# Moving three batches' attention epilogue and router into the second attention's loop, with a fixed memory region per expert

## The reference

```python
x = x + _L0_xattn_ref(_layernorm(x), ctx, mask)
x = x + _L0_ffn_ref(_layernorm(x), ...)      # 16 experts, top 6
x = x + _L1_xattn_ref(_layernorm(x), ctx, mask, Wq, ..., residual_scale)
x = x + _L1_ffn_ref(_layernorm(x), ...)      # 16 experts, top 2
```

```python
probs = softmax(clip(q @ k.T / 4))           # 16 heads of 16
ctx = (probs @ v).reshape(B, S, H)
delta = rs * (ctx @ Wo.T + bo)
delta = (delta - mean) / sqrt(var + 1e-5) * ln_gamma + ln_beta
...
logits = flat @ router_w.T
scores = softmax(logits)
_, topk_idx = top_k(logits + router_bias, 2)
# topk_scores normalised to sum 1; for every expert e:
#   out += combine[:, e] * ((silu(flat @ Wu[e]) * (flat @ Wg[e])) @ Wd[e])
# and the shared expert: silu(flat @ Su) * (flat @ Sg) @ Sd
```

## Times and profile before

| | us |
|---|---|
| median of 3 runs | 824.03 |
| lowest, highest | 823.6, 827.82 |
| profiled execution | 823.29 |
| its span in the trace | 821.4 |
| PE / DVE / ACT / POOL busy | 704.0 / 537.9 / 396.3 / 127.8 |

### The profile page before, as it was taken

One profiled execution on the slowest core, in us unless ns is written; L12 is line 12 of the kernel. 1 busy time (PEld: TensorE's weight loads), 2 busy tenths in 40 slices (PEclk: granted clock), 3 DMA queues, 4 the chain that ended last, 5 costly groups with the idle time before them and its releaser, 6 DMA issues.

```text
span 821.4 us, 14394 instructions
## 1 busy us (share of the span) xinstructions
PE 704.0 (86%) x5463; PEld 533.1 (65%) x5463; DVE 537.9 (65%) x1080; ACT 396.3 (48%) x555; POOL 127.8 (16%) x109
## 2 busy tenths in 40 slices
PE   5799999896869999999994699999999984675990
PEld 4689888796658888888884344444444444564880
DVE  6765665666676666666676377777777768563553
ACT  2624233333322223333222599999999981223540
POOL 6452625030000000000000000000000002062651
PEclk9999999998989999999998699999999997896995
DMA  7465554635305334343368289999997209023545
GB/s 228 131 220 196 165 217 150 243 113 192 68 22 135 116 91 131 90 120 103 109 131 189 46 171 140 143 145 200 166 220 143 37 2 345 0 75 104 163 138 179
DMA packets 66456, 114.59 MB, mean 139 GB/s; under 512 B 15984, under 2 KB 44272, under 8 KB 65376
## 3 DMA queue, kind: packets, MB, share of 16 engines
q1 hardware_dynamic: 63136, 106.40, 52.1%
q0 software_dynamic: 2256, 6.18, 2.2%
q10 hardware_dynamic: 1008, 1.25, 0.5%
HBM read 78.93 MB, written 31.75 MB: 135 GB/s over the span
## 4 chain that ended last, share of the span: by engine, by line
PE 51%; ACT 17%; DVE 12%; issue 10%; DMA 5%; POOL 2%; SPq 2%; another core or an unknown queue 1%; POOLq 0%; ACTq 0%; DVEq 0%
ACT p L1155 13%; PE ps L602 12%; PE ps L603 12%; PE ps L604 12%; PE ps L976 3%; PE ps L856 2%; PE ps L838 2%; DMA raw<-in_ctxN 2%; PE ps L990 2%; DMA raw<-in_ctxT 2%; PE ps L614 1%; ACT cNh L1054 1%; POOL cTl L574 1%; DVE st L1204 1%; DMA k_lo<-kl 1%
## 5 line engine op out<-in xcount | busy, mean ns | idle before, releaser
L1155 ACT ACTIVATE p<-ps,kbias 128x1024 f32<-128x1024 f32 (+1 forms) x208 | 208.7, 1426 | 1.1 <-PE ps L838 1.1
L1535 DVE TENSOR_SCALAR p<-p 128x1024 f32<-128x1024 f32 (+1 forms) x208 | 144.2, 693 | 57.9 <-ACT p L1155 56.4
L856 PE MATMUL ps<-p,vsl 128*17 128x256 f32 (+1 forms) x1664 | 113.6, 387 | 0.7 <-DVE p L1535 0.7
L838 PE MATMUL ps<-qst,kst 48*128 48x256 f32 (+1 forms) x832 | 99.7, 328 | 14.4 <-DMA qst<-ql 5.9
L838 PEld LDWEIGHTS ps<-qst,kst 48*128 48x128 f32 (+1 forms) x832 | 60.9, 186 | 75.7 <-ACT p L1155 46.3
L1117 ACT ACTIVATE hh<-h 128x512 fp32r<-128x512 f32 x50 | 31.6, 632 | 138.5 <-DVE h L1467 114.7
L602 PE MATMUL ps<-xTh,w_hi 128*128 128x512 f32 x200 | 79.9, 400 | 5.2 <-DVE h L1463 4.4
L604 PE MATMUL ps<-xTh,w_lo 128*128 128x512 f32 x200 | 79.4, 397 | 0.0
L603 PE MATMUL ps<-xTl,w_hi 128*128 128x512 f32 x200 | 79.3, 396 | 0.0
L583 POOL CAST sh_hi<-e_w 128x768 fp32r<-128x768 f32 x2 | 1.7, 828 | 469.0 <-DMA e_w<-in_w 469.0
L856 PEld LDWEIGHTS ps<-p,vsl 128*17 128x17 f32 (+1 forms) x1664 | 37.7, 97 | 37.8 <-issue 4.3
(11 more groups left out here) (277 smaller groups left out, 1464.9 us busy)
## 6 DMA issues: line engine op xcount, KB each, us to landing
kst<-k_hi SPq DMA_DIRECT2D x64, 200.2 KB, 9.0
w_raw<-in_w SPq DMA_DIRECT2D x25, 384.0 KB, 3.1
v_one<-vst SPq DMA_DIRECT2D x4, 1768.0 KB, 9.2
vsl<-v_one SPq DMA_DIRECT2D x4, 1768.0 KB, 16.2
kst<-k_lo SPq DMA_DIRECT2D x32, 200.2 KB, 8.7
raw<-in_ctxN SPq DMA_DIRECT2D x12, 512.0 KB, 5.8
k_hi<-kh SPq DMA_DIRECT2D x24, 256.0 KB, 2.6
k_lo<-kl SPq DMA_DIRECT2D x24, 256.0 KB, 2.9
```

Source lines behind the costliest of these rows:

```text
L838: mm = pe.matmul(ps[0:rows, 2 * (x % RING) + t, c * SEQ:(c + 1) * SEQ], kst[r, job % KSL, c, m * P:m * P + rows], qst[r, b, 2 * g + c, :], ...
L856: mm = pe.matmul(ps[32 * j:32 * j + VW, 6 + job % 2, 0:SEQ], vsl[0:rows, b % 2, at_:at_ + VW], p32[0:rows, x % PBUF, (2 * t + c) * SEQ:(2 ...
L1155: act.activation(p32[0:rows, x % PBUF, :], psf[0:rows, bank * 512:bank * 512 + 1024], ACT.Exp, scale=0.25, bias=kbias[0:rows, col:col + 1] ...
L1535: dve.tensor_scalar(t, t, CLO, CHI, ALU.max, ALU.min).then_inc(p_clip, 1)
```

## The change

For batches 0 to 2 the work between `cx` and the router moves into the loop of the following batch. Functions `between` on TensorE, ScalarE and VectorE put a piece of it at fixed steps `o` of the 52 steps of a batch (`UB`), in the free half of a PSUM bank; `free_again` keeps the attention's products from overwriting it. The router of batch `b` follows one batch later. In the loop GpSimd computes 1/sqrt(var + eps) by three Newton steps from an integer guess (`inverse_root`), so that ScalarE keeps its table. After the loop stand batch 3 (tiles 6 and 7), the logits of batch 2, and the router of tiles 4 to 7.

Rows go to a region of 1024 rows per expert (`CAP`, `first_row`), so that a position doesn't need the other experts' counts: the scatters of batches 0 and 1 (8 of 16) are in the loop. `x_slots` grows from 3968 to 20480 rows; all of it is filled with empty rows beforehand, by 20 DMAs in the first FFN instead of 12 in the loop. Each block's row in memory (`rb_i`) is worked out by five more linked instructions and read into a register by SyncE. The output projection takes fp32 operands as they are, in one matmul where it was three of fp32r. `norm` comes two steps earlier.

```diff
-NORM_AT = 7
+NORM_AT = 5
...
+CAP = NB * SEQ
+NFILL = E + -(-NBLK * P // CAP)
+UB = NG * MT
...
+        def inverse_root(e, b, n):
+            s = slice(2 * b, 2 * b + 2)
...
+            y, yi = rguess[:, s], rguess[:, s].bitcast(I32)
+            link(e.tensor_scalar(nv[:], mv[:, s, 1], EPS, None, ALU.add))
+            link(e.tensor_scalar(yi, nv[:].bitcast(I32), -0.5, 1597463007.0, ALU.mult, ALU.add))
+            for k in range(3):
+                link(e.tensor_tensor(na[:], nv[:], y, ALU.mult))
+                link(e.tensor_tensor(na[:], na[:], y, ALU.mult))
+                link(e.tensor_scalar(na[:], na[:], -0.5, 1.5, ALU.mult, ALU.add))
+                if k < 2:
+                    link(e.tensor_tensor(y, na[:], y, ALU.mult))
+            e.tensor_tensor(rstd[:, s], na[:], y, ALU.mult).then_inc(rs_rdy, 1)
...
@@ SyncE, first FFN
+                    if 1 <= r <= NFILL:
+                        sp.dma_start(xs_d[(r - 1) * CAP:r * CAP, :].rearrange("(p k) d -> p k d", p=P), blank[:]).then_inc(x_zero, 16)
...
@@ SyncE, attention loop
-                if KSL + NG < job <= KSL + NG + 4:
-                    empty_slots(job - KSL - NG - 1)
...
@@ SyncE, slots_in
-                sp.dma_start(xb[:, j % XR, :], xs_d[j * P:(j + 1) * P, :]).then_inc(xb_in[j % XR], 16)
+                row = sp.value_load(rb_i[0:1, j:j + 1], min_val=0, max_val=NFILL * CAP - P)
+                sp.dma_start(xb[:, j % XR, :], xs_d[bass.ds(row, P), :]).then_inc(xb_in[j % XR], 16)
...
@@ GpSimd, beside the attention loop
+            for b in range(NB - 1):
+                pool.wait_ge(dl_mv, 2 * b + 2)
+                inverse_root(pool, b, 0)
+                pool.wait_ge(ln_mv, 3 * NT + 2 * b + 2)
+                inverse_root(pool, b, 1)
+                if b:
+                    rows_out(b, 2 * b - 2, 2 * b)
...
@@ TensorE, loop
+            def between(y):
+                b, o = y // UB - 1, y % UB
...
+                if 0 < b < NB - 1 and o == 36:
+                    ranks(b, t - 2, t, spare)
+                if 0 < b < NB - 1 and o == 10:
+                    logits(b - 1, spare)
+                if 0 <= b < NB - 1:
+                    if o == 13 - 1:
+                        ctx_T(t, 2, spare)
+                    elif o == 23:
+                        ctx_out(t, 0, 2, spare[:, 0:D])
+                    elif o == 24:
+                        ctx_out(t + 1, 1, 2, spare[:, D:2 * D])
+                    elif o == 49:
+                        rows_T(t, 2, spare)
...
@@ ScalarE, loop
+                    if o == 12:
+                        ctx_ev(t, 2, spare)
+                    elif o == 49:
+                        rows_hi(t, 2, spare)
...
@@ ScalarE, after the loop
+            act.activation(std[:, 0:1], eps[:], ACT.Sqrt)
...
+            act.activation(std[:, 0:1], eps[:], ACT.Silu)
+            for j in range(2):
+                rows_hi(t + j, 1, ps[:, 4 + j, :])
...
@@ VectorE, loop: at o = 25 delta, 27 and 28 its statistics, 30 and 32 gamma
+                    elif o == 34:
+                        delta_add(t)
+                    elif o == 35:
+                        delta_add(t + 1)
+                    elif o == 36:
+                        rows_stat(t)
+                    elif o == 37:
+                        rows_stat(t + 1)
+                    elif o == 39:
+                        rows_mean(b)
+                    elif o == 43:
+                        rows(t)
+                    elif o == 45:
+                        rows(t + 1)
+                    elif o == 50:
+                        rows_lo(t, 2, spare)
...
@@ VectorE, after the first shared chunk
+            link(dve.tensor_tensor(big_d[:], big_d[:], nblk_[:].unsqueeze(1).broadcast_to([P, NBLK, E]), ALU.mult))
+            link(dve.tensor_reduce(ob[:], big_d[:], AX.X, ALU.add))
+            link(dve.tensor_tensor(ob[:], blk[:], ob[:], ALU.subtract))
+            link(dve.scalar_tensor_tensor(out=rb_f[:], in0=eb_f[:], scalar=float(CAP // P), in1=ob[:], op0=ALU.mult, op1=ALU.add))
+            dve.tensor_scalar(rb_i[:], rb_f[:], float(P), None, ALU.mult).then_inc(eb_rdy, 1)
```

More of the change, by code:

```diff
@@ L510, in _ @@
             sp.wait_ge(slots_out, 16 * 2 * NT)
+            sp.wait_ge(eb_rdy, 2)
             def slots_in(j):
@@ new lines, in ranks @@
+            def ranks(n, t0, t1, o):
+                pe.wait_ge(sel_rdy, n)
+                pe.wait_ge(tri_rdy, 2)
+                pe.matmul(o[:, 0:(t1 - t0) * E], upper[:], sel[:, t0:t1, :].rearrange("p t e -> p (t e)"), start=True, stop=False, skip_group_check=True)
+                for t in range(t1 - 1):
+                    u = max(t + 1, t0)
+                    mm = pe.matmul(o[:, (u - t0) * E:(t1 - t0) * E].rearrange("p (t e) -> p t e", e=E), ones[:], sel[:, t:t + 1, :].broadcast_to([P, t1 - u, E]),
+                                   start=False, stop=t == t1 - 2, skip_group_check=True)
+                mm.then_inc(pre_rdy, 1)
@@ new lines, in delta_mean, with delta_gamma, delta_add @@
+            def delta_mean(b):
+                dve.wait_ge(dl_st, 2 * b + 2)
+                for t in (2 * b, 2 * b + 1):
+                    dve.bn_aggr(mv[:, t, :], st6[:, t, :]).then_inc(dl_mv, 1)
+            def delta_gamma(t):
+                dve.wait_ge(dl_mv, t + 1)
+                dve.scalar_tensor_tensor(out=dlt[:, t, :], in0=dlt[:, t, :], scalar=mv[:, t, 0:1], in1=gam[:], op0=ALU.subtract, op1=ALU.mult).then_inc(dl_g, 1)
+            def delta_add(t):
+                dve.wait_ge(rs_rdy, t // 2 * 2 + 1)
+                dve.wait_ge(dl_g, t + 1)
+                dve.wait_ge(beta_rdy, t + 1)
+                dve.scalar_tensor_tensor(out=resid[:, t, :], in0=dlt[:, t, :], scalar=rstd[:, t:t + 1], in1=resid[:, t, :], op0=ALU.mult, op1=ALU.add).then_inc(dl_r, 1)
@@ new lines, in rows_stat, with rows_mean, rows @@
+            def rows_stat(t):
+                dve.wait_ge(dl_r, t + 1)
+                dve.bn_stats(st6[:, t, :], resid[:, t, :]).then_inc(ln_stat, 1)
+            def rows_mean(b):
+                dve.wait_ge(ln_stat, 3 * NT + 2 * b + 2)
+                for t in (2 * b, 2 * b + 1):
+                    dve.bn_aggr(mv[:, t, :], st6[:, t, :]).then_inc(ln_mv, 1)
+            def rows(t):
+                dve.wait_ge(rs_rdy, t // 2 * 2 + 2)
+                if t == 0:
+                    dve.wait_ge(q_in[NG], 16 * 3 * HG * NG)
+                    dve.wait_ge(d_cst, 16 * 10)
+                    dve.tensor_copy(xe[:, :, D + 1], tok[:]).then_inc(xe_rdy, 1)
+                dve.tensor_scalar(xe[:, t, 0:D], resid[:, t, :], mv[:, t, 0:1], rstd[:, t:t + 1], ALU.subtract, ALU.mult).then_inc(ln_xn, 1)
@@ L1631, in _ @@
-            dve.tensor_tensor(sel[:], one1[:], one2[:], ALU.add).then_inc(sel_rdy, 1)
-            dve.wait_ge(pre_rdy, 1)
-            cnt = ps[:, 6, NT * E:NT * E + E]
+            b, t = NB - 1, NT - 2
+            for j in range(2):
+                delta(t + j, 1, ps[:, 2 + j, :])
+                delta_stat(t + j)
+            delta_mean(b)
+            delta_gamma(t)
+            delta_gamma(t + 1)
+            dve.wait_ge(rg_rdy, 1)
+            dve.reciprocal(rstd[:, t:NT], std[:, t:NT]).then_inc(rs_rdy, 1)
@@ new lines, in _ @@
+            delta_add(t)
+            delta_add(t + 1)
+            rows_stat(t)
+            rows_stat(t + 1)
+            rows_mean(b)
+            dve.wait_ge(rg_rdy, 2)
+            dve.reciprocal(rstd[:, t:NT], std[:, t:NT]).then_inc(rs_rdy, 1)
+            rows(t)
+            rows(t + 1)
+            for j in range(2):
+                rows_lo(t + j, 1, ps[:, 4 + j, :])
+            logits_ev(t - 2, NT, ps[:, 7, :])
+            biased(t - 2, NT)
+            max_equal(t - 2, NT)
+            max_first(t - 2, NT, one1)
@@ L1759 @@
         "tok": np.arange(NB * SEQ, dtype=np.float32).reshape(NT, P).T,
-        "empty": np.stack([np.full((P, NBLK), 100.0, np.float32), (NB * SEQ + np.arange(NBLK * P, dtype=np.float32)).reshape(NBLK, P).T], axis=2),
+        "first_row": np.tile(np.arange(E, dtype=np.float32) * CAP, (P, 1)),
+        "aside": (NROW + np.arange(NBLK * P, dtype=np.float32)).reshape(NBLK, P).T,
         "upper": np.triu(np.ones((P, P), np.float32), 1),
```

402 lines of the change are left out of this document (247 added, 155 removed).

## The result

The changed kernel takes 816.9 us (median of 4 runs, 815.9 to 818.8) against 825.9 of the kernel before in the same rounds: a ratio of 0.9887, 95% interval 0.9862 to 0.9912. So it is faster by about 1%, 7 to 9 us, where 19 were forecast. The profiled execution took 816.0 with a span of 814.2.

What follows compares the result with a forecast made beforehand. Bounds: ScalarE's exponentials in the second attention's loop, then a 71.4 us serial chain to the experts. Profiled 823.3 - 27.4 (tail) + 8.5 (loop) = 804.4, predicted as 805 us; range 796 to 818.

Steps and rivals of the forecast that it cites:

- rival 1: Loop: VectorE's clips starve GpSimd's inverse root, costing 6 to 12 us in three batches; 812 us; 0.30 together with rival 2.
- I add 1.5: Loop: VectorE's two waits per batch for GpSimd's inverse root, taken as 3.9 us long, cost 1.5 us in all.
- rival 2: Tail: the 6.73 us wait of unknown releaser before the residual add stays; 812 us; 0.30 together with rival 1.
- the cast slowed from 0.67 to 1.07: Kernel's first microseconds: GpSimd cast took 1.07 us beside VectorE, 0.67 without; cited as evidence for rival 1.
- ScalarE's 3.6: Loop: six copies of 128x512 at 0.60 us each, unhidden because ScalarE is the bound, add 3.6 us.
- TensorE's 3.4: Loop: lumps of projections, logits and context transposes overrun the ring of three score buffers, adding 3.4 us.
- gamma 6.2 and add 7.3: Tail: last batch's gamma ends 6.2 us after the loop's end, reciprocal and add 7.3, at 0.34 to 0.41 per VectorE instruction.
- The 16 zero matmuls and the chunk ahead of the ranks, 1.9 + 2.8: Tail: TensorE's zero matmuls take 1.9 us and 12 shared-chunk matmuls 0.23 each, so it reaches the ranks at 18.0.
- up to 3 us for the clock: Tail: up to 3 us may be lost if TensorE is at 1.2 GHz while the shared chunk runs.
- From the positions on: Tail: positions at 20.8 us, then scatters beside shared expert, softmax weights and residual adds; experts start at 44.0.
- Rival 3: First FFN: empty-row fills exceed the 5.0 us free per tile period, costing 26 us; 831 us; chance 0.07.
- Rival 4: More gain: loop costs only ScalarE's 3.6 us and the tail ends 3 us sooner; 797 us; chance 0.08.

Runs made afterwards that it cites:

- e1: Changed kernel with GpSimd's inverse root of the first three batches replaced by a plain multiply: 812.0 us, 0.981 of before; loop 219.8 us.
- e9: Changed kernel with VectorE's statistics, means, adds and rows moved by one or two steps, whole root kept: 811.7 us, 0.983 of before; loop 220.3 us.
- e6: Changed kernel with the inverse root replaced by a multiply and ScalarE's six loop copies cut to 2 or 4 columns: 809.6 us, 0.978; loop 217.6 us.
- e2: Changed kernel with GpSimd's split of the shared weights held until the last normalized rows are written: 814.1 us, 0.986 of before; tail 47.0 us.
- e3: Changed kernel with the 16 zero matmuls issued earlier, where TensorE idles ahead of the last row transposes: 815.5 us, 0.987 of before; tail 46.5 us.

## Why the prediction was wrong

The direction and the range hold (816.9 in 796 to 818), the gain does not: 9 us instead of 19. That the range holds is in part luck: it let the loop run to 22 over before and took the tail as worked out, and the tail was 6.3 us longer. The prediction's own signs said so too: from the first exponential to the end of the last one 222.8 us (205 to 220 foreseen), a tail of 50.3 (42 to 47), and 3.1 us a batch of VectorE idle for rstd, where over 2 was to mean rival 1. By its own steps:

*The loop's "I add 1.5" for the two waits for GpSimd.* This step failed. They cost 7.1 (e1) or 6.7 (e9), 5.7 by the means of six loops each. I priced the root at 3.9 us from uncontended links; it took 5.2 to 6.5 beside the clips, while the rows were asked for after 4. That is rival 1 in kind, and in size (6 to 12 us in three batches), though not in its arithmetic: it had one link per clip and 5.0 us of waits a batch, and the trace has about two links per clip and 3.1 us. I gave it and rival 2 together 0.30. The row that spoke for it, the cast slowed from 0.67 to 1.07, was less to the point than I wrote: the slow one stood beside a VectorE instruction with two SBUF inputs (L1325), not beside a clip, and VectorE worked beside the fast one too (L1312, L1317, L1319). I let VectorE's own waiting outweigh it. That waiting did free GpSimd (the second roots took 5.2 to 5.5 us, the first 6.3 to 6.5), but not enough.

*ScalarE's 3.6 and TensorE's 3.4* were right: 3.8 of copies in the trace, and 3.1 (e6). With the 7.1 they make 14.1 of loop, where it grew by 14.0.

*The tail's gamma 6.2 and add 7.3.* This step failed too: the pairs took 5.2 us together instead of 1.8. I had weighed GpSimd against VectorE for the loop and not for the tail, where GpSimd splits the shared weights at the same moment. In the kernel before, the split was over at 687.0 and gamma began at 690.7. Price 3.4 (e2).

*The 16 zero matmuls and the chunk ahead of the ranks, 1.9 + 2.8.* They took 3.65 + 4.6 at the lower clock, 3.5 more. I had named up to 3 us for the clock and not put it in the sum. I had also named 50 us as the point from which links or clock failed; the tail took 50.3. e3 shows that 3.8 us could be had by issuing the zeros in TensorE's idle time.

From the positions on the steps hold: 22.6 us from there to the experts, forecast 23.2. The wait of 6.73 did not stay, so rival 2 falls; the links follow each other (end of the last weight 738.49, add 738.51):

```profile
738.31 0.18 DVE m_w L1930
738.49 0.02 issue
738.51 2.49 DVE resid L1934 x4
```

Rival 3 falls by the tile period of 8.30. A fill landed in 6.0 us; less the 1.9 of a small write that is 4.1 for its data, where I had estimated 4.3 and 5.0 were free. Rival 4 did not come.

The sum with the measured terms: 804.4 + 5.6 (root, 7.1 instead of 1.5) + 3.4 + 3.5 = 816.9, where the profiled execution took 816.0; the tail by it is 50.9, measured 50.3.

## What to carry to other kernels

Work that goes to an engine next to another one's stream must be priced contended, at every place where the two meet, and asked for after its worst time, not its best: here moving statistics, adds and rows by one or two steps gave back about 6 us without removing an instruction. When a long serial stretch is shortened, look at what used to hide in its gaps (a weight split, zero fills), since it now stands beside or ahead of the path; and expect that a gain ahead of it can cost it something, as here the clock. When a placing test fails, look for the waits that the test itself added before believing its rival.
